# One more tile of lag between the stages of an expert loop (mixture of experts inside an attention kernel, one core)

## The reference

```
gate_weights = softmax(x @ gate_w + gate_b)            # 8 experts
topk_vals, topk_idx = top_k(gate_weights, 2)
h = gelu(x @ w1[e] + b1[e])                            # 128 -> 256
h = gelu(h @ w2[e] + b2[e])                            # 256 -> 256
expert_out = h @ w3[e] + b3[e]                         # 256 -> 128
out = sum over the 2 chosen experts of topk_vals * expert_out
```

## Time and profile before

| | |
|---|---|
| median of 3 runs | 727.19 us (727.04 to 727.5) |
| the profiled execution | 733.76 us |
| its span, first to last instruction | 732.0 us |
| mean granted TensorE clock | 0.967 |
| PE busy | 632.8 us (86%) |
| ACT busy | 563.0 us (77%) |
| DVE busy, POOL busy | 196.7 us, 211.4 us |
| expert stage, first layer 1 to first scores of the attention behind it | 344.92 to 508.61 us |

### The profile page before, as it was taken

One profiled execution on the slowest core, in us unless ns is written; L12 is line 12 of the kernel. 1 busy time (PEld: TensorE's weight loads), 2 busy tenths in 40 slices (PEclk: granted clock), 3 DMA queues, 4 the chain that ended last, 5 costly groups with the idle time before them and its releaser, 6 DMA issues.

```text
span 732.0 us, 13577 instructions
## 1 busy us (share of the span) xinstructions
PE 632.8 (86%) x4256; PEld 268.6 (37%) x4256; DVE 196.7 (27%) x521; ACT 563.0 (77%) x696; POOL 211.4 (29%) x218
## 2 busy tenths in 40 slices
PE   7499999979788888888999999998888888888885
PEld 3224322222222222222888888887122222222221
DVE  5763353563113211101112122121020221202214
ACT  3389989968888879998444444445799999999995
POOL 2400062037636744440111111111433323333310
PEclk9789999999899989999999999999799999999999
DMA  6671052124213422152566666664121212212214
GB/s 202 201 309 64 17 152 79 44 74 135 91 68 104 129 78 73 58 147 70 171 186 188 186 187 193 181 188 125 43 61 53 64 43 68 68 44 56 52 35 117
DMA packets 70547, 80.60 MB, mean 110 GB/s; under 512 B 7008, under 2 KB 50944, under 8 KB 70512
## 3 DMA queue, kind: packets, MB, share of 16 engines
q1 hardware_dynamic: 63968, 66.17, 29.6%
q0 software_dynamic: 5968, 13.51, 7.1%
q10 hardware_dynamic: 576, 0.45, 0.2%
HBM read 50.81 MB, written 29.29 MB: 109 GB/s over the span
## 4 chain that ended last, share of the span: by engine, by line
PE 47%; ACT 22%; issue 18%; ACTq 5%; DVE 4%; DMA 2%; another core or an unknown queue 1%; SPq 0%; POOL 0%; DVEq 0%
ACT probs L542 19%; PE ps L1109 18%; PE ps L1142 11%; PE ps L1094 8%; PE ps L1063 3%; ACTq L554 3%; ACT work L558 2%; PE ps L1118 2%; DVE o_sb L745 1%; PE ps L1134 1%; PE ps L1152 1%; DMA q_st<-q_d 1%; PE ps L1022 1%; ACTq L538 1%
## 5 line engine op out<-in xcount | busy, mean ns | idle before, releaser
L542 ACT ACTIVATE probs<-ps 128x1024 f32<-128x1024 f32 x512 | 481.0, 1042 | 49.5 <-PE ps L1094 38.0
L1109 PE MATMUL ps<-probs,v_st 128*32 128x512 f32 x2048 | 282.7, 625 | 56.2 <-ACT probs L542 31.0
L1094 PE MATMUL ps<-q_st,k_st 24*128 24x512 f32 x1024 | 133.5, 510 | 13.6 <-ACT probs L542 8.1
L558 ACT ACTIVATE work<-ps,b 128x256 f32<-128x256 f32 x156 | 69.7, 473 | 92.5 <-PE ps L1142 69.0
L1094 PEld LDWEIGHTS ps<-q_st,k_st 24*128 24x128 f32 x1024 | 50.7, 187 | 237.8 <-ACT probs L542 194.7
L480 POOL DMA_INDIRECT work<-slots_y_d,slot_i x64 | 60.4, 944 | 125.7 <-PE ps L1109 113.6
L1109 PEld LDWEIGHTS ps<-probs,v_st 128*32 128x32 f32 x2048 | 41.6, 109 | 140.9 <-ACT probs L542 87.1
L1142 PE MATMUL ps<-work 128*128 128x256 f32 x312 | 76.6, 388 | 10.6 <-ACT work L558 10.4
L440 POOL DMA_INDIRECT slots_x_d<-xn_all,slot_i x64 | 61.8, 965 | 62.3 <-PE ps L1109 49.3
L463 POOL DMA_DIRECT2D slots_y_d<-work x39 | 27.9, 715 | 157.2 <-DVE work L856 152.3
L745 DVE COPY o_sb<-ps 128x512 f32<-128x512 f32 x32 | 22.1, 691 | 174.0 <-PE ps L1109 165.7
(11 more groups left out here) (129 smaller groups left out, 299.1 us busy)
## 6 DMA issues: line engine op xcount, KB each, us to landing
work<-in_L_ffn_w_dram SPq DMA_DIRECT2D x78, 128.0 KB, 2.3
work<-in_L_ffn_w_dram SPq DMA_DIRECT2D x39, 256.0 KB, 3.0
k_st<-k_d SPq DMA_DIRECT2D x32, 256.0 KB
q_st<-q_d SPq DMA_DIRECT2D x32, 256.0 KB
slots_x_d<-zeros SPq DMA_DIRECT2D x10, 512.0 KB, 6.9
work<-slots_x_d SPq DMA_DIRECT2D x40, 128.0 KB, 2.6
slots_y_d<-work POOLq DMA_DIRECT2D x39, 128.0 KB, 2.5
k_d<-part_hi SPq DMA_DIRECT2D x16, 256.0 KB
```

The lines of the kernel that those rows point to most:

```text
L542: nc.scalar.activation(probs[:, j % PROB_RING, 2 * pair:2 * pair + 2, :], score_slot(j, pair).rearrange("p (h n) -> p h n", h=2), ACT.Exp, ...
L558: ins = nc.scalar.activation(dst[:, par, k, :], src[k][:, 0:ST], ACT.Gelu, bias=bias[:, bass.ds(e, 1), k])
L1094: ins = nc.tensor.matmul(score_slot(j, h // 2)[:, (h % 2) * HALF:(h % 2 + 1) * HALF], k_st[32 * h:32 * h + ROWS, mt * P:(mt + 1) * P], q_s ...
L1109: ins = nc.tensor.matmul(o_ps[32 * h:32 * h + 32, :], v_st[:, mt, h, :], probs[:, j % PROB_RING, h, :], start=(mt == 0), stop=(mt == MT - 1))
```

## The change

Each stage of the expert loop is moved so that its iteration has layer 1 of tile j+2, layer 2 of j+1, layer 3 of j and the transposition of j+3, in this order. Since layer 2 of a tile now follows the next tile's layer 1, layer 1 waits also for the GELU that frees `h1_ps`, and layer 2 for the one that frees `h2_ps`. ACT's GELUs are split in two functions with a value load each. DVE does `finish_y(j)` and then `copy_xsT(j+3)`. SP issues w1, w2, w3 and rows, each of the three weights with a value load of its own. The loops run one iteration (two tiles) less, and what is over is written out ahead of them and behind them. The 40th row tile, which was loaded and transposed and used for nothing, is dropped.

```
             load_rows(2, 0)
+            load_rows(3, 1)
             load_w1(2, 0, expert_of(2))
+            load_w1(3, 1, expert_of(3))
+            load_rows(4, 0)
             load_w2(2, 0, expert_of(2))
-            with sp.Fori(0, (SLOT_TILES - 3) // 2) as i:
-                load_rows(i * 2 + 3, 1)
-                e = expert_of(i * 2 + 3)
-                load_w1(i * 2 + 3, 1, e)
-                load_w3(i * 2 + 2, 0)
-                load_w2(i * 2 + 3, 1, e)
...
+            with sp.Fori(0, (SLOT_TILES - 5) // 2) as i:
+                for k in range(2):
+                    load_w1(i * 2 + (4 + k), k, expert_of(i * 2 + (4 + k)))
+                    load_w2(i * 2 + (3 + k), 1 - k, expert_of(i * 2 + (3 + k)))
+                    load_w3(i * 2 + (2 + k), k)
+                    load_rows(i * 2 + (5 + k), 1 - k)
...
+            gelu1(0, 0)
+            gelu1(1, 1)
+            gelu2(0, 0)
+            with act.Fori(0, (SLOT_TILES - 3) // 2) as i:
+                gelu1(i * 2 + 2, 0)
+                gelu2(i * 2 + 1, 1)
+                gelu1(i * 2 + 3, 1)
+                gelu2(i * 2 + 2, 0)
+            gelu1(SLOT_TILES - 1, 0)
+            gelu2(SLOT_TILES - 2, 1)
+            gelu2(SLOT_TILES - 1, 0)
...
-            with dve.Fori(1, (SLOT_TILES - 1) // 2) as i:
+            copy_xsT(4, 0)
+            with dve.Fori(1, (SLOT_TILES - 3) // 2) as i:
                 for par in range(2):
-                    copy_xsT(i * 2 + (2 + par), par)
                     finish_y(i * 2 + par, par)
-            finish_y(SLOT_TILES - 1, 0)
+                    copy_xsT(i * 2 + (3 + par), 1 - par)
+            for j in range(SLOT_TILES - 3, SLOT_TILES):
+                finish_y(j, j % 2)
...
             def layer1(j, par):
                 pe.wait_ge(w1_in[par], in_count(j, par))
                 pe.wait_ge(S["xsT_made"], j + 1)
+                if not isinstance(j, int) or j > 0:
+                    pe.wait_ge(S["g1_done"], j)
...
-            def layer2(j, par):
+            def layer2(j, par, first=False):
                 pe.wait_ge(w2_in[par], in_count(j, par))
                 pe.wait_ge(S["g1_done"], j + 1)
+                if not first:
+                    pe.wait_ge(S["g2_done"], j)
...
             layer1(0, 0)
             turn(SPLIT - 1, 1)
-            layer2(0, 0)
+            layer1(1, 1)
+            turn_rows(2, 0)
+            layer2(0, 0, first=True)
             free_aux(len(AUX))
-            with pe.Fori(0, (SLOT_TILES - 1) // 2) as i:
+            with pe.Fori(0, (SLOT_TILES - 3) // 2) as i:
                 for k in range(2):
-                    layer1(i * 2 + (1 + k), 1 - k)
-                    turn_rows(i * 2 + (2 + k), k)
+                    layer1(i * 2 + (2 + k), k)
+                    layer2(i * 2 + (1 + k), 1 - k)
                     layer3(i * 2 + k, k)
-                    layer2(i * 2 + (1 + k), 1 - k)
-            pe.wait_ge(S["xsT_made"], SLOT_ROOM)
+                    turn_rows(i * 2 + (3 + k), 1 - k)
+            last_tile = SLOT_TILES - 1
+            layer1(last_tile, 0)
+            layer2(last_tile - 1, 1)
+            layer3(last_tile - 2, 0)
+            layer2(last_tile, 0)
+            layer3(last_tile - 1, 1)
+            pe.wait_ge(S["xsT_made"], SLOT_TILES)
             pe.wait_ge(S["g1_done"], SLOT_TILES)
             scores(SPLIT, 0, first=True)
-            layer3(SLOT_TILES - 1, 0)
+            layer3(last_tile, 0)
```

More of the change, by code:

```diff
@@ L343, in _ @@
             load_rows(2, 0)
+            load_rows(3, 1)
             load_w1(2, 0, expert_of(2))
+            load_w1(3, 1, expert_of(3))
+            load_rows(4, 0)
             load_w2(2, 0, expert_of(2))
[L346 to L358 removed]
+            with sp.Fori(0, (SLOT_TILES - 5) // 2) as i:
[4 more added lines that the diff above has]
+                    load_rows(i * 2 + (5 + k), 1 - k)
+            for j in range(SLOT_TILES - 1, SLOT_TILES + 2):
+                if j < SLOT_TILES:
+                    load_w1(j, j % 2, expert_of(j))
+                if j - 1 < SLOT_TILES:
+                    load_w2(j - 1, (j - 1) % 2, expert_of(j - 1))
+                load_w3(j - 2, j % 2)
             for t in range(SPLIT, STEPS - 1):
@@ L551, in _, with gelu1, gelu2 @@
                 attention_exps(t)
-            def gelus(j, par):
+            def gelu1(j, par):
                 e = act.value_load(expert_i[0:1, bass.ds(j, 1)], min_val=0, max_val=E_ - 1)
[L555 to L559, removed]
+                for k in range(2):
+                    act.wait_ge(S["l1_done"], j * 2 + (k + 1))
+                    ins = nc.scalar.activation(h1[:, par, k, :], h1_ps[k][:, 0:ST], ACT.Gelu, bias=b1_sb[:, bass.ds(e, 1), k])
+                ins.then_inc(S["g1_done"], 1)
+            def gelu2(j, par):
+                e = act.value_load(expert_i[0:1, bass.ds(j, 1)], min_val=0, max_val=E_ - 1)
+                for k in range(2):
+                    act.wait_ge(S["l2_done"], j * 2 + (k + 1))
+                    ins = nc.scalar.activation(h2[:, par, k, :], h2_ps[k][:, 0:ST], ACT.Gelu, bias=b2_sb[:, bass.ds(e, 1), k])
+                ins.then_inc(S["g2_done"], 1)
             act.wait_ge(S["routed"], 2)
             act.wait_ge(S["wT_copied"], 3)
[L563 to L566, removed]
+            gelu1(0, 0)
[9 more added lines that the diff above has]
+            gelu2(SLOT_TILES - 1, 0)
             nc.scalar.activation(fb[:, 3:4], zeros[:, 0:1], ACT.Exp)
```

## The result

The changed kernel takes 751.53 us (median of 4 runs, 747.81 to 756.39), the kernel before 727.12 us (4 runs): ratio 1.0342, 95% interval 1.0271 to 1.0413, so slower by 24.4 us. The runs of the changed kernel lie 8.6 us apart and sort by the mean granted clock of the run: 0.981, 0.975, 0.970 and 0.967 at 747.81, 748.83, 754.23 and 756.39 us. The profiled execution is the first of them (span 746.0 us).

The account below looks back on a forecast made before the run. It took ACT's register load in a ring with layer 2 to bound the kernel; the new ring through DVE, 2.67 + 1.26 + 0.33 + 0.42 + 0.15 = 4.83 us a tile, gave +21.8 us, 749.0 us, own range 743.6 to 754.0, eight in ten 741 to 758.

Parts of the forecast that it names:

- The bound before: Expert stage before the change: 4.19 us a tile against 3.91 without waiting, so 0.28 us a tile of waiting, about 10 us.
- a ring with layer 2: PE and ACT before the change: layer 2, GELU, register load, GELU, layer 2; 2.57 + 0.54 + 0.84 + 0.15 = 4.10 us.
- the tile that waited for nothing: Start of the expert stage before: layer 1 at 353.83 to the next at 357.74, taken as PE's own 3.91 us.
- The transposition's hand-over decides: Transposition to DVE's copy to layer 1 has no lag, behind `finish_y`: PE waits every tile, about 0.9 us.
- The ring's terms: New loop: layers 1 and 2, layer 3 to addition, addition to copy, copy, release of layer 1; 4.83 us a tile.
- SP: SP's issue queue with three value loads a tile: 4.60 us, hidden under 4.83 by 0.23 us a tile.
- Start and end: Around the loop: first loop layer 1 at 350.91; 7.68 us from layer 1 of tile 38 to the attention's exponentials.
- I cost the transfers at nothing: SP's loads in the new order: each of the four keeps its lead, so transfers add 0 us.
- The sum: Whole shift: 36 x 4.83 - 152.1 = +21.8 us, reaching the kernel's end in full.
- HAM oscillation — how this bites in real kernels: Rival, chance 0.10: PE's clock falls in the stage; two slow tiles give 756, a quarter of them about 782 us.
- A faster kernel: Rival, chance 0.04: copy ready when layer 1 asks and SP's queue fits; 3.91 us a tile, -11.3 us, 715.9.
- SP was not the bound: Rival that SP's queue is the bound, chance 0.07: 4.60 us a tile, +13.5 us, 740.7.

Follow-up runs that it names:

- act_loads: Kernel before the change, with only ACT's loads of the expert's number moved out of the ring: 3.92 us a tile, 714.45 us against 727.8 (0.9813).
- act_loads_sp: Kernel before, ACT's expert loads moved out of the ring, and three SP expert loads in two tiles instead of four: 3.72 us a tile, 700.46 us against 715.91.
- swap_dve: Changed kernel with DVE's loop order exchanged, `copy_xsT` ahead of `finish_y`: 4.49 us a tile, 739.9 us against 727.8 (1.0161).
- turn_late_alone: Kernel before, with only the transposition moved to the body's end and DVE's addition ahead of its copy, no added lag: 4.58 us a tile against 4.20.
- turn_early_sp: Changed kernel, transposition right behind layer 1, DVE's copy ahead of its addition, four SP expert loads in two tiles instead of six: 4.05 us a tile, 724.34 us against 727.8.
- after_sp_less: Changed kernel with four SP loads of the expert's number in two tiles instead of six, nothing else: 4.76 us a tile, stage 189.6 us.
- turn_early: Changed kernel with the transposition right behind layer 1 and DVE's copy ahead of its addition: 4.53 us a tile, 739.56 us against 727.8 (1.0154).
- after_sp_more: Changed kernel with one more SP value load per tile, loaded and not used: 5.10 us a tile, stage 198.2 us.
- after_again: Changed kernel run once more, unaltered, for the scatter of the stage's start: start 7.4 us, 4.76 us a tile, stage 186.3 us.

## Why the prediction was right, point by point

*The bound before.* Right in the mechanism: ACT's register load stood in a ring with layer 2. act_loads takes it out of the ring and leaves PE, DVE and SP as they were, and a tile falls from 4.20 to 3.92 us. The size was off: I took the tile that waited for nothing from the earlier trace rows as 3.91 us, but the same instructions take 3.70 once the GELUs come earlier (act_loads_sp). Part of the difference is a wait ahead of that tile's layer 2 that no matmul's record shows, but the weight load's time does:

```profile
354.91 1.06 PE L1152 MATMUL ps<-work 128*128 128x128 f32 x8
354.95 0.84 ACT L558 ACTIVATE work<-ps,b 128x256 f32<-128x256 f32 x2 [0.35 <-PE ps L1134]
...
355.90 1.59 PEld L1142 LDWEIGHTS ps<-work 128*128 128x128 f32 x8
355.93 1.97 PE L1142 MATMUL ps<-work 128*128 128x256 f32 x8
```

ACT's GELUs end at 355.79 and the weight load of layer 2 starts at 355.90. From layer 3 to layer 2 it is 1.02 us here and 0.89 in act_loads_sp (402.33 to 403.22). The other 0.08 us lies between layer 2 and the next layer 1 (1.81 against 1.73 us) and is not explained. The order before had 0.5 us a tile to give, not 0.28, about 18 us in all.

*The transposition's hand-over decides.* Right, and shown four ways: the timeline of the changed kernel, swap_dve (the addition's part, 0.27 us), turn_late_alone (the hand-over alone, 0.39 us in the old loop), and turn_early_sp against after_sp_less, which have the same SP loop: with the hand-over covered a tile takes 4.05 us, with it exposed 4.76.

*The ring's terms.* Forecast 2.67 + 1.26 + 0.33 + 0.42 + 0.15 = 4.83, measured 4.763: layers 1 and 2 2.69 (401.28 to 403.97), layer 3 to the addition 1.22 in this tile and 1.30 in the next (408.69 to 409.99), so 1.26 as forecast, addition to copy 0.34, copy 0.41, end of copy to layer 1 0.06. They add up to 4.76. The term that was off is the last: I had taken ACT's 0.15 for DVE's. It makes 36 x (4.763 - 4.83) = -2.4 us. The 0.34 us between the starts of two operations of 0.42 agrees with the pair of copies in the earlier trace rows, not with the waiting for an empty pipeline that the Trainium skill's page "VectorE: DVE Perf Modes" describes in "The DRAIN you can't avoid". The same section adds that a next operation that is not held starts earlier, which the forecast left out; no run here tells which of its two cases this is.

*SP.* Right that it is hidden, and by little: fewer loads change nothing, more loads bring 5.10 us. The 4.60 us was too high: where SP is the bound (turn_early) a tile takes 4.53, and swap_dve ran at 4.49. A register load is worth 0.49 us between turn_early and turn_early_sp (one fewer a tile) and 0.57 from turn_early to after_sp_more, a kernel with one more a tile, not 0.65.

*Start and end.* This step failed in its size. The forecast let layer 1 of tile 2 start 5.99 us after that of tile 0 (344.92 to 350.91); it took 8.90 us, as long as before. It had costed the earlier transposition's transfer at nothing. The term "I cost the transfers at nothing" held in the loop, where the lead of each load is what it was, but the transposition of tile 2 was moved forward by a whole layer and its rows were not there. That is +2.9 us, of which 1.23 is the wait for the rows, and 1.2 the slow layer 2 (3.15 - 1.97); most of the rest is layer 1 of tile 1 and the transposition, which also took longer from start to start.

The slow part did not come in every execution. Seven traces have this start. In four of them (after_again, after_sp_more, swap_dve, turn_early) the clock stayed at 1.00, PE waited 1.17 to 1.48 us for the rows, and the start took 7.4 to 7.7 us. In three (the changed kernel, turn_early_sp, after_sp_less) the clock fell to 0.5 and the start took 8.9 to 9.9 us. So what comes with the change each time is 1.4 to 1.7 us over the forecast, and the fall, where it comes, another 1.5 us (8.90 against 7.39 us in the same kernel). The end was 7.58 us (520.34 to 527.92) for the 7.68 forecast.

*The sum.* 21.8 - 2.4 + 2.9 - 0.1 = 22.2 us; the stage grew from 165.8 to 187.9 us, by 22.1. Two errors of opposite sign made the total look better than its terms, and that is luck: after_again, the same kernel without the fall of the clock, has a stage of 186.3 us, 20.5 more than before. The medians moved by 24.4 us; its interval (5.2 us to either side) holds the forecast's 21.8 as well as both of these.

*The rivals.* The clock stayed at 1.00 in the loop, with 0.75 to 0.84 us of waiting in each tile; the case that the Trainium skill's page "TensorE: Matmul & The Clock Gate" tells in "HAM oscillation — how this bites in real kernels" did not come about, at these waits. A faster kernel would have needed a wait under 0.31 us ahead of layer 1. SP was not the bound: after_sp_less changed nothing.

## What to carry to other kernels

When a software pipeline gets more lag, write down for every hand-over what now stands between producer and consumer: here two (layer 1 to layer 2, layer 2 to layer 3) got more and one, transposition to copy to layer 1, was left with nothing between, and DVE's written order put an unrelated operation into it. Before adding lag, look at what the short ring consists of; a register load moved by a few lines gave 13 us where the lag lost 24. Then count the register loads of the queue that issues the transfers: it was the next bound in turn_early and in act_loads, and showed itself there as late data, not as a busy engine.

## What the runs showed of the hardware

- A load of a table entry into a register costs SP's queue about half a microsecond (0.49 and 0.57 us a tile for one), nearly the 0.58 us from one issue to the next without a load.
- Where DVE's copy released PE, the next matmul started 0.06 us after its end (405.94 to 406.00); where ACT's GELU did, 0.15 us. It goes with the engine that releases rather than with the layer: layer 1 of tile 1 in the changed kernel, released by ACT's GELUs, started 0.14 us after their end (342.99 to 343.13). Why is open.
- A matmul group without a recorded idle time can still have waited: groups of layer 2 that showed no idle time made 3.91 us tiles, and the same instructions ran in 3.70. The time from one layer's first matmul to the next one's shows it (1.02 against 0.89 us from layer 3 to layer 2).
- A granted clock of 0.52 came after 1.50 and 1.23 us of waiting close together, and the 8 matmuls of a layer 2 took 3.15 us instead of 1.97. The length of the waits alone does not decide: the clock also fell after 1.50 and 1.07 us in turn_early_sp, and it stayed at 1.00 after 1.50 and 1.48 us in turn_early.
